# First narrow attention layer: the first eight heads' transposes move ahead of the next batch's scores

## The reference, cut to what matters

```python
q = (x @ Wq + bq).reshape(B, Tx, HEADS, HEAD_DIM).transpose(0, 2, 1, 3)
k = (xf @ Wk + bk).reshape(B, Txf, HEADS, HEAD_DIM).transpose(0, 2, 1, 3)
v = (xf @ Wv + bv).reshape(B, Txf, HEADS, HEAD_DIM).transpose(0, 2, 1, 3)
scores = jnp.einsum('bhqd,bhkd->bhqk', q * SCALE, k)
probs = jax.nn.softmax(scores, axis=-1)
attn = jnp.einsum('bhqk,bhkd->bhqd', probs, v)
out = attn.transpose(0, 2, 1, 3).reshape(B, Tx, D) @ Wo + bo
```

## Time and profile before

| | us |
|---|---|
| median of 3 runs | 1740.02 (1736.38 to 1742.77) |
| the profiled execution | 1737.04 |
| its span in the trace | 1735.3 |
| of it, from the scores of the first batch to the last y of this layer | 851.6 to 1067.0 |
| PE busy in the span | 1632.6 (94%) |
| DVE busy | 1315.0 (76%) |
| ACT busy | 1244.4 (72%) |

### The profile page before, as it was taken

How to read it: one execution, slowest core, us unless ns; L and a number is a source line. 1 busy time by engine, 2 the same in 40 slices (tenths; PEclk the granted TensorE clock), 3 DMA queues, 4 the chain that set the end, 5 groups by cost and what they waited for, 6 DMA issues and landing times. The chain is left out here.

```text
span 1735.3 us, 48956 instructions
## 1 busy us (share of the span) xinstructions
PE 1632.6 (94%) x16520; PEld 1349.1 (78%) x16520; DVE 1315.0 (76%) x2408; ACT 1244.4 (72%) x3858; POOL 677.3 (39%) x946
## 2 busy tenths in 40 slices
PE   7999999999999999889899998978999999999997
PEld 6888888788888888779677777867787878787875
DVE  5777777777777777747588886656888888888885
ACT  4777777677777777623488886446888888888885
POOL 3444444454444444423222222633343434343431
PEclk9999999999999999999999999999999999999999
DMA  6777777777777667720000000013434343444441
GB/s 193 198 188 185 190 193 190 212 208 204 195 185 188 188 186 187 207 76 0 1 2 0 0 0 1 1 53 123 135 113 136 113 136 114 128 121 121 129 133 50
DMA packets 230717, 216.30 MB, mean 125 GB/s; under 512 B 19874, under 2 KB 228324, under 8 KB 230628
## 3 DMA queue, kind: packets, MB, share of 16 engines
q1 hardware_dynamic: 230628, 215.17, 44.7%
HBM read 112.34 MB, written 102.76 MB: 124 GB/s over the span
## 5 line engine op out<-in xcount | busy, mean ns | idle before, releaser
L658 ACT ACTIVATE L_probs<-L_scores,L_neg_max 128x128 f32<-128x128 f32 x512 | 182.7, 386 | 133.7 <-DVE L_neg_max L740 133.7
L854 POOL TENSOR_TENSOR L_probs<-L_probs,L_inv_sum 128x1024 f32<-128x1024 f32 x128 | 242.8, 1897 | 87.7 <-DVE L_inv_sum L760 87.7
L734 DVE TENSOR_REDUCE L_row_max<-L_scores 128x8 f32<-128x1024 f32 x128 | 156.2, 1220 | 42.4 <-PE L_scores L534 42.4
L1947 POOL TENSOR_TENSOR L2L_w_probs<-L2L_w_probs,L2L_w_inv_sum 128x1024 f32<-128x1024 f32 x64 | 121.4, 1896 | 156.1 <-DVE L2L_w_inv_sum L1774 156.1
L766 DVE STREAM_TRANSPOSE L_squares<-L_probs 128x1024 f32<-128x1024 f32 x128 | 156.7, 1224 | 0.3 <-POOL L_probs L854 0.3
L581 PE MATMUL L_ring<-L_probsT,L_v 128*64 128x128 f32 x2048 | 127.4, 276 | 10.1 <-issue 10.1
L581 PEld LDWEIGHTS L_ring<-L_probsT,L_v 128*64 128x64 f32 x2048 | 110.8, 137 | 30.5 <-issue 28.6
L534 PE MATMUL L_scores<-L_kT,L_qT 64*128 64x128 f32 x2048 | 131.8, 278 | 0.9 <-ACT L_kT L647 0.9
L534 PEld LDWEIGHTS L_scores<-L_kT,L_qT 64*128 64x128 f32 x2048 | 119.4, 188 | 12.5 <-ACT L_oT L647 8.2
L750 DVE TENSOR_REDUCE L_sums<-L_probs 128x8 f32<-128x1024 f32 x64 | 78.1, 1220 | 65.2 <-ACT L_probs L665 65.2
L1571 ACT ACTIVATE L2L_w_probs<-L2L_scores,L2L_w_neg_max 128x128 f32<-128x128 f32 x256 | 90.3, 370 | 45.6 <-DVE L2L_w_neg_max L1738 45.6
(11 more groups left out here) (220 smaller groups left out, 4610.8 us busy)
## 6 DMA issues: line engine op xcount, KB each, us to landing
L_relay<-L_squares SPq DMA_DIRECT2D x128, 512.0 KB, 3.4
L_probsT<-L_relay SPq DMA_DIRECT2D x512, 128.0 KB, 3.6
L2L_relay<-L2L_w_squares SPq DMA_DIRECT2D x64, 512.0 KB, 3.5
L2L_w_probsT<-L2L_relay SPq DMA_DIRECT2D x256, 128.0 KB, 2.9
out_x<-x SPq DMA_DIRECT2D x32, 64.0 KB, 2.8
L0a_wq<-in_L_xattn_Wq SPq DMA_DIRECT2D x2, 256.0 KB, 3.0
L0a_wk<-in_L_xattn_Wk SPq DMA_DIRECT2D x2, 256.0 KB, 3.9
L0a_wv<-in_L_xattn_Wv SPq DMA_DIRECT2D x1, 512.0 KB, 6.5
```

The source lines that it names most:

```text
L658: done = nc.scalar.activation(slot_probs(at, 0)[:, n, :], scores[:, 0, r, i, :], ACT.Exp, scale=layer_of(at).scale, bias=neg_max[:, n:n + ...
L734: nc.vector.tensor_reduce(row_max[:, s, :], slot(s), AX.X, ALU.max).then_inc(max_ready[s], 1)
L854: nc.gpsimd.tensor_tensor(to, to, inv_sum[:, :, s, :].unsqueeze(3) .to_broadcast([TOKENS, 2, GROUP, TOKENS]), ALU.mult).then_inc(divided, 1)
L1947: nc.gpsimd.tensor_tensor(to, to, w_inv_sum[:, :, s, :].unsqueeze(3) .to_broadcast([TOKENS, 2, GROUP, TOKENS]), ALU.mult).then_inc(w_divid ...
```

## The change

In `step` of PE, the scores of the next batch move behind the transposes T0 and T1 of this batch. Nothing else is changed: no instruction is added or taken away, and the other engines' programs are the same.

```diff
             def step(t):
-                if here(t, 1):
-                    score(t.plus(1))
                 if here(t, 0):
                     transpose_probs(t, 0)
                     transpose_probs(t, 1)
+                if here(t, 1):
+                    score(t.plus(1))
                 if here(t, -1):
                     project_out(t.plus(-1))
                 if here(t, 0):
```

## The result

| | before | after |
|---|---|---|
| median of 13 runs each, us | 1740.72 (1736.38 to 1742.77) | 1745.83 (1744.50 to 1752.17) |
| ratio to before | | 1.0038 (95% interval 1.0029 to 1.0048) |
| span of the profiled execution, us | 1735.3 | 1743.1 |

The account below looks back on a forecast made before the run. It took a loop of waits through ACT to bound the kernel, replaced by a 6.81 us loop through DVE's copy of the values; 6.6 us added to 1740.02 gave 1746.6 us, likeliest 1742 to 1750, wider 1739 to 1752.

Parts of the forecast that it names:

- The bound before: Steady steps of the old kernel: 6.52 us each, a loop of waits through ACT's exponentials, scores, T0 and ACT's copies.
- What was taken away: ACT's 0.96 us wait at the copies can go; its loop eases by about 0.9 us and no longer bounds.
- The loop that was added: Row maxima to DVE's copy of the values, T0, T1, scores, next maxima: 4.535 + 0.05 + 1.02 + 1.20 = 6.81 us.
- The step that turned on the changeover of the array: PE from T0 to scores: 1.09 us of transposes less 0.07 overlap at the change of array cut, 1.02 us.
- B: Rival on PE's passage from T0: scores 0.93 us behind it, gains at both ends, 1743.1 us; chance 0.17.
- C: Rival on PE's passage from T1 to scores: no overlap plus register instructions, 1751.1 us; chance 0.22.
- The sum: Maxima of batch 1 to batch 31: 202.6 us against 196.46, costing 6.1 us plus 0.5 for occasional waits, 6.6.
- The start: Scores of batch 1 at the layer's start: some 0.3 us later; effect from -0.5 to +0.6 us, taken as 0.
- now waits about 1 us in front of T0: PE in a steady step: its wait of about 0.5 us for the scores becomes about 1 us before T0.
- PE idle 0.7 to 1.1 us before it: Sign in the later profile's steady steps: T0 released by DVE's copy of the values, PE idle this long before it.
- rival A: Bank wait at T0 met early, eased ACT loop counts: step falls to DVE's 6.08 us, total 1728.6; chance 0.06.
- D: Rival on the clock: PE's idle 1 us a step lowers it, 21 us over 30 steps, 1768 us; chance 0.03.

Follow-up runs that it names:

- e3: Kernel before the change with one spare DVE instruction per step ahead of the copy of the values; ratio to before 1.0001, median 1739.79 us.
- e7: Kernel before the change with DVE's copies of values and transposed rows moved ahead of the subtraction of slot 1; ratio to before 1.0002, median 1740.23 us.
- e1: Changed kernel with one spare DVE instruction per step just ahead of the copy of the values; ratio to before 1.0108, median 1758.21 us.
- e2: Changed kernel with one spare DVE instruction per step behind the copies of values and transposed rows; ratio to before 1.0040, median 1746.54 us.
- e4: Changed kernel with DVE's copies of values and transposed rows moved ahead of the subtraction of slot 1; ratio to before 1.0003, median 1740.02 us.
- e5: Changed kernel with T0 alone ahead of the scores and T1 moved back behind them; ratio to before 0.9965, median 1733.17 us.

## Why the prediction was right, point by point

**The bound before.** A loop over ACT's exponentials, scores, T0 and ACT's copies, with air on DVE. That DVE was not on it is shown by e3 and e7, where DVE's work and order could be changed for nothing. The loop itself rests on its sum: 0.05 + 1.07 + 0.70 + 2.18 + 0.30 + 2.19 = 6.49 us, as far as the scores' starts lie apart in the earlier trace rows (956.93 to 963.42). No run changed ACT's part alone.

**What was taken away.** ACT no longer waits for T0's copy; it waits 1.28 us for T2's instead, as said. Slot 0 is raised 5.60 us behind the scores' start (955.00 to 958.41 + 2.19 = 960.60), as forecast. Eased and of no use, since ACT no longer sets the step.

**The loop that was added.** T0 was released by the copy of the values, as forecast, and e1 with e2 shows that the work ahead of the copy, and not DVE's work in all, is paid. The terms, forecast and measured: 4.47 and 4.60 for DVE's part, measured the same (the 4.60 holds the 0.18 us pause before y, so it is not all work); T0 to scores 1.02, measured 1.02 (960.73 to 961.75) and 0.99 (967.71 to 968.70); scores to maxima 1.20, measured 1.21; release of T0 0.05, measured 0.05 in one of the loop's steps and 0.15 in the other (967.56 to 967.71). This later start in every second step is most of the difference between 6.81 forecast and 6.85 measured. Its cause is not isolated: in the steps that are written out T0 carries two waits, for the bank and for the exponentials, and in the loop's first step only the one for the bank; perhaps the loop's second step is like the former.

The step that turned on the changeover of the array held: the records of T0 and T1 end at 960.73 + 1.09 = 961.82, the scores begin at 961.75, 0.07 us before. "TensorEngine Tiling (Array Packing)" of the Trainium skill, in Tiling Modes, Key Properties, says that a change of tiling mode drains the engine. This trace shows a price in that sense, but a small one: the scores start 1.02 us behind T0, where a projection of the same cut started 0.93 behind it, and 0.07 of overlap between the records stayed. The ends of matmul records are modelled by the profile, so the distances of starts are the firmer reading. Rivals B and C, which put this passage at 0.93 and from 1.10 on, are out.

**The sum.** The row maxima of batches 1 and 31 are now at 860.89 and 1065.15, 204.26 us apart, against 196.46: 7.8 more, where I had 6.1 and 0.5 for odd waits, 6.6. The 0.04 us a step in 24 steady steps make 1.0. The first turn of the loop has one step of 7.23 us (880.50 to 887.73) instead of 6.81, with a pause of 0.47 us before y, and the four steps outside the loop come to 25.86 us instead of 25.72; these two make 0.6, for which the 0.5 had been set aside. The start, taken as 0 between -0.5 and +0.6, came out at the upper end: the maxima of batches 0 and 1 are 7.29 us apart (853.60 to 860.89) against 6.70 (852.80 to 859.50). The timeline of the start:

```profile
857.11 0.66 PE L987 MATMUL L_ring<-ident,L_probs 128*128 128x128 f32 x4 [2.61 <-ACT L_probs L1066]
...
858.73 2.09 PE L975 MATMUL L_scores<-L_k_apart,L_qT 32*128 32x512 f32 x8
```

```profile
858.00:861.00 3.00, 2.85 (x13) 1.19 (x14) 0.78 (x4) 2.12 (x4) 0.00 (x0) 0.62 0.00 0
```

The scores of batch 1 began 0.3 us later against the first maxima, as I had reckoned. The hope that the clock would be up again by then failed: they fell almost whole into the time of the lower clock (granted 0.62 in the mean of these 3 us) and took 2.09 us where it had been 1.84. At the end the last y comes 10.56 us behind the last maxima (1065.15 to 1075.71) instead of 10.77. The layer is thus 0.59 + 7.80 - 0.21 = 8.2 us longer in the profiled execution. The ratio puts the whole kernel at 6.6 us, with an interval of 5.0 to 8.4, so the two agree. That the forecast of 0.38% was met to the last digit is luck: by the trace the layer lost 8.2 us where the sum had 6.6, the start and the steady steps both being taken too low.

**What was wrong.** The step that spoke of PE's wait, "now waits about 1 us in front of T0", failed, and with it the sign "PE idle 0.7 to 1.1 us before it". Measured were 0.37 us at T0 and 0.45 at the values matmul in one kind of step, 0.43 and 0.58 in the other: about 1 us in all, but in two places. I had moved the projection, T2, T3, queries and keys 0.83 us earlier and did not ask for whom the values matmul, behind them, would then have to wait: its bank holds the projection until y is written, and before the change PE came there late enough. This second wait was hidden behind the first and so did not change the sum: 2.41 us behind the values matmul, as in e4, T0 could have started at 958.14 + 2.41 = 960.55, and the copy let it go at 960.73. It makes rival A wrong in its size as well: had T0 not needed the copy early, the step would have been 6.60 (e4) and the time that of the kernel before, and not 11 us less.

**The other rivals.** Rival A's mechanism did not occur: T0 was held by the bank. Nor did D's: with PE's waits of up to 0.6 us at a time the granted clock in the steady stretch stayed at 1.00.

## What to carry to other kernels

When an instruction is moved ahead on an in-order engine, list its waits, ring buffers' above all, and add up the new loop from the releasing engine back to itself; an engine that waits an eighth of its time can be the bound by where in its step the releasing instruction stands. Everything that moves earlier behind it reaches its own waits earlier too, so the same count is due for these. Move the least that feeds the waiting engine: here four transposes ahead of the scores gained 0.35%, eight lost 0.38%.

## What the runs showed of the hardware that I had not expected

- In every second step T0, held by the copy, loaded its weights 0.11 us and started 0.15 us behind the release (967.56 to 967.67 and 967.71); in the other steps both came 0.05 behind it (960.68 to 960.73). e1 and e5 show the same two values to 0.01 us. The number of waits on the instruction may be the reason; no run isolated it.
- The granted clock fell to 0.50, its lower level (1.2 of 2.4 GHz), near the start of the layer, where PE had been idle for 2.61 us and T0 and T1 of batch 0 came right behind; before the change it had idled 3.91 us there. It stood at 1.00 until 858 us and at 0.50 from 859 to 862. Doing work earlier did not keep the clock up.
- The changeovers of the array's cut without a wait in them (scores to T0 in the kernel before, 958.07 to 958.00; T1 to scores after, 961.82 to 961.75) show the same 0.07 us of overlap with the last record.
